# A Mamba-MLP block and a ternary FFN on one core: where the low bits of the FFN weights are summed, and how the last tile ends

## The reference

```python
def block(x):                       # first half
    xn = rmsnorm(x)
    z, xbc, dt_raw = split(xn @ w_in)            # 512, 768, 8 columns
    xc = silu(conv1d_4_taps(xbc) + conv_b)       # xh (512), B (128), C (128)
    dt = softplus(dt_raw + dt_bias)
    a = dt * -exp(a_log)
    # chunks: within a chunk masked exp(segsum(a)) * (C B^T) @ (dt*xh),
    # between chunks a state [heads, 64, 128] with decay
    y = y_diag + y_off + d_skip * xh
    g = rmsnorm(y * silu(z)) * norm_w
    h = x + g @ w_out
    return h + square(relu(rmsnorm(h) @ w_fc)) @ w_proj
def ffn(x):                         # ternary weights times scales per output row
    h = silu(w1(x)) * w2(x)         # 256 -> 1024
    h = gelu(h1(h)); h = gelu(h2(h))  # 1024 -> 1024, twice
    return w3(h)                    # 1024 -> 256
x = layernorm(x + block(x))
return layernorm(x + ffn(x))
```

## Time and profile before

| | |
|---|---|
| median of three timed executions | 1258.24 us (1256.99 to 1261.23) |
| the profiled execution, its own time | 1263.54 us |
| span in that profile | 1261.59 us |
| TensorE busy | 1209.6 us (96%) |
| VectorE busy | 797.7 us (63%) |
| ScalarE busy | 643.5 us (51%) |
| GpSimd busy | 249.8 us (20%) |
| mean granted clock of TensorE | 0.988 |

### The profile page before, as it was taken

The page is one execution under the profiler, slowest core; times in us unless marked ns, Lnnn a source line. Parts: engine busy times, 40 slices in busy tenths (PEclk is TensorE's granted clock), DMA queues, the critical chain, the costliest instruction groups (busy, mean ns, idle before and its releaser), DMA issues.

```text
span 1261.6 us, 19157 instructions
## 1 busy us (share of the span) xinstructions
PE 1209.6 (96%) x6452; PEld 1014.9 (80%) x6452; DVE 797.7 (63%) x1399; ACT 643.5 (51%) x1232; POOL 249.8 (20%) x215
## 2 busy tenths in 40 slices
PE   6779999999999999989999999999999999999996
PEld 4567887878787888878888888888888888888885
DVE  6898898988888898974624536336354263452633
ACT  5758787878787887756414214133241241422410
POOL 0445344342616253530000000000000000000000
PEclk9889999999999999999999999999999999999998
DMA  8111303131222220213800100101001010010000
GB/s 301 52 63 41 111 19 94 57 110 56 88 78 87 71 85 33 102 34 108 337 1 1 34 1 4 29 0 33 0 0 33 0 33 0 0 33 0 17 1 18
DMA packets 31112, 68.37 MB, mean 54 GB/s; under 512 B 3936, under 2 KB 22496, under 8 KB 29152
## 3 DMA queue, kind: packets, MB, share of 16 engines
q1 hardware_dynamic: 31072, 67.84, 15.7%
HBM read 59.43 MB, written 22.03 MB: 65 GB/s over the span
## 4 chain that ended last, share of the span: by engine, by line
issue 52%; POOL 0%; DVE 0%; POOLq 0%; DVEq 0%
POOL rsv_b L1771 0%; DVE o_sb L1842 0%; POOLq L1769 0%; DVEq L1623 0%; POOL rsv L234 0%; POOLq L434 0%
## 5 line engine op out<-in xcount | busy, mean ns | idle before, releaser
L1757 ACT ACTIVATE full<-bank,scale 128x512 f32<-128x512 f32 x128 | 88.3, 690 | 384.0 <-PE bank L1669 384.0
L1669 PE MATMUL bank<-hB_lo,h_sb 128*128 128x512 f32 x512 | 200.2, 391 | 0.0
L1669 PE MATMUL bank<-hB_hi,h_sb 128*128 128x512 f32 x512 | 199.7, 390 | 0.0
L1669 PE MATMUL bank<-hA_hi,h_sb 128*128 128x512 f32 x512 | 199.3, 389 | 0.0
L1669 PE MATMUL bank<-hA_lo,h_sb 128*128 128x512 f32 x512 | 199.3, 389 | 0.0
L1817 DVE CAST hA_hi<-full 128x512 fp32r<-128x512 f32 x64 | 27.3, 427 | 185.8 <-ACT full L1757 185.8
L1771 POOL TENSOR_TENSOR rsv_b<-mv_b,eps 128x4 f32<-128x4 f32 x8 | 10.7, 1339 | 624.9 <-DVE mv_b L186 624.9
L1669 PEld LDWEIGHTS bank<-hA_lo,h_sb 128*128 128x128 f32 x512 | 96.1, 188 | 20.1
L1669 PEld LDWEIGHTS bank<-hA_hi,h_sb 128*128 128x128 f32 x512 | 96.1, 188 | 20.1
L1669 PEld LDWEIGHTS bank<-hB_hi,h_sb 128*128 128x128 f32 x512 | 96.2, 188 | 19.2
L1669 PEld LDWEIGHTS bank<-hB_lo,h_sb 128*128 128x128 f32 x512 | 96.2, 188 | 19.1
(11 more groups left out here) (214 smaller groups left out, 3035.9 us busy)
## 6 DMA issues: line engine op xcount, KB each, us to landing
chk_xh<-w_ffn SPq DMA_DIRECT2D x16, 704.0 KB, 4.1
ffn_raw<-w_ffn SPq DMA_DIRECT2D x8, 1408.0 KB, 8.0
h_sb<-ffn_raw SPq DMA_DIRECT2D x2, 4096.0 KB, 19.5
xT<-x_t SPq DMA_DIRECT2D x8, 512.0 KB, 4.8
x_res<-x SPq DMA_DIRECT2D x8, 512.0 KB, 3.9
x_rows<-x SPq DMA_DIRECT2D x8, 512.0 KB, 3.4
x_in<-x_rows SPq DMA_DIRECT2D x8, 512.0 KB, 4.4
out<-o_sb SPq DMA_DIRECT2D x8, 512.0 KB, 3.2
```

The costliest lines, as they stand in the source:

```text
L1669: ins = pe.matmul(o, a_, b_, start=first and n == 0, stop=last and n == 1, skip_group_check=True)
L1757: nc.scalar.activation(full[:, n % FULL, :], b[:], ACT.Gelu, scale=scale[:, 1 + n // KH, n % KH:n % KH + 1]).then_inc(s_gd, 1)
```

## The change

VectorE's `low_bits` and its semaphore are gone. ScalarE's `low_sum` reads the low 16 bits of each word itself, as an unsigned 16-bit view with a stride of two over a whole half (128 x 1408), waits for the DMA of the half, and is called twice a pass: before yT(1), after the first projection of xbc, and before fc(7), after gate_rms(2). Each sum covers what four instructions (two masks, two sums) did. The sum now takes 16 low bits where 12 were masked before. `load_half` waits for one sum per half instead of two. lowsum has 16 columns instead of 32.

For the last tile of the FFN, TensorE issues the last two channels (j = 6, 7) of w3 first for chunks 0 and 1 and then for 2 and 3; `finish_last` of VectorE takes each accumulator as it is ready; and SyncE stores the last tile in two DMAs of two chunks each. `layer_norm_tail` is the old layer norm without its first part, split out so that `finish_last` can call it.

```diff
 def load_half(n, at):
-    ge(sp, s_sum, 2 * n)
+    ge(sp, s_sum, n)
     sp.dma_start(chk, w_ffn[:, bass.ds(at, PART)]).then_inc(s_chk, 16)
...
 def low_sum(i, n):
-    act.wait_ge(s_low, CHECKS * i + n + 1)
-    part = chk[:, n % HALVES * LOW:(n % HALVES + 1) * LOW]
-    nc.scalar.activation(part, part.bitcast(I32), ACT.Copy,
-                         accum_out=lowsum[:, bass.ds(CHECKS * i + n, 1)]).then_inc(s_sum, 1)
+    act.wait_ge(s_chk, 16 * HALVES * i + 16 * n + 16)
+    part = chk.bitcast(U16).rearrange("p (n b) -> p n b", b=2)[:, :, 0]
+    nc.scalar.activation(part, part, ACT.Copy,
+                         accum_out=lowsum[:, bass.ds(HALVES * i + n, 1)]).then_inc(s_sum, 1)
...
-def low_bits(i, n):
-    if n % HALVES == 0:
-        dve.wait_ge(s_chk, 32 * i + 16 * (n // HALVES) + 16)
-    part = chk[:, n % HALVES * LOW:(n % HALVES + 1) * LOW].bitcast(I32)
-    nc.vector.tensor_scalar(part, part, LOW_BITS, None,
-                            ALU.bitwise_and).then_inc(s_low, 1)
...
 store(TILES - 2, (TILES - 2) * TILE * D)
-store(TILES - 1, (TILES - 1) * TILE * D)
-sp.wait_ge(s_store, 16 * TILES + 1)
+i = TILES - 1
+for n in range(2):
+    r = slice(2 * n, 2 * n + 2)
+    sp.wait_ge(s_o, CH * i + 2 * n + 2)
+    sp.dma_start(rows(out, i * TILE * D)[:, r, :], o_sb[:, r, :]).then_inc(s_store, 16)
+sp.wait_ge(s_store, 16 * (TILES + 1) + 1)
...
-for j in range(KH - BEHIND, KH):
-    out_rows(j)
+if more:
+    for j in range(KH - BEHIND, KH):
+        out_rows(j)
+else:
+    for j in range(KH - BEHIND, KH - 2):
+        out_rows(j)
+    for half in (range(0, CH // 2), range(CH // 2, CH)):
+        for j in range(KH - 2, KH):
+            out_rows(j, half)
...
+def finish_last(i):
+    step = Steps(dve, s_bstep, B_STEPS * i)
+    dve.wait_ge(s_store, 16 * i + 1)
+    for n in range(2):
+        r = slice(2 * n, 2 * n + 2)
+        o = o_sb[:, r, :]
+        dve.wait_ge(s_acc, KH * i + KH + 2 * n)
+        nc.vector.tensor_tensor(o, acc[n][:].rearrange("p (c n) -> p c n", c=2),
+                                s3_b[:].unsqueeze(1).broadcast_to([P, 2, D]), ALU.mult).then_inc(s_accd, 1)
+        dve.wait_ge(s_accd, 2 * i + n + 2)
+        step.link(nc.vector.tensor_tensor(o, o, x1_res[:, r, :], ALU.add))
+        for c in range(2 * n, 2 * n + 2):
+            step.mark(nc.vector.bn_stats(bn_b[:, c, :], o_sb[:, c, :]))
+    step.wait(step.n)
+    layer_norm_tail(step, bn_b, mv_b, EPS_LN).then_inc(s_mvb, 1)
...
```

More of the change, by code:

```diff
@@ L22 @@
 BF16 = mybir.dt.bfloat16
+U16 = mybir.dt.uint16
 ALU = mybir.AluOpType
@@ L45 @@
 EPS_LN = 1e-05
-LOW_BITS = 0xFFF
 FAR = 1e30
@@ L99 @@
 FFN_WORDS = (2 * KD + 2 * KH) * HID + KH * D
-CHECKS = 4
 class Where:
@@ L140, in post_ln_block @@
     PART = PIECE // HALVES
-    LOW = PIECE // CHECKS
-    assert PIECE * TILES == FFN_WORDS and LOW * CHECKS == PIECE and CHECKS == 2 * HALVES
+    assert PIECE * TILES == FFN_WORDS and PART * HALVES == PIECE
     w_head, w_first = Where(HEAD, 0, ()), Where(FIRST, 0, (HEAD,))
@@ L178, in layer_norm_stats, with layer_norm_tail @@
             step.wait(step.n)
+            return layer_norm_tail(step, bn, mv, eps)
+        def layer_norm_tail(step, bn, mv, eps):
             tt, ts = nc.vector.tensor_tensor, nc.vector.tensor_scalar
@@ L259, in post_ln_block @@
         eps = sb("eps", [P, 4])
-        lowsum = sb("lowsum", [P, TILES * CHECKS])
+        lowsum = sb("lowsum", [P, TILES * HALVES])
         low_all = sb("low_all", [P, 1])
@@ L420, in post_ln_block @@
         s_raw = sem("ffn_piece_stored")
-        s_low = sem("low_bits_ready")
         s_sum = sem("low_bits_summed")
@@ L990, in iteration @@
                     yT(w, 0)
-                    low_sum(i, 0)
                     if more:
@@ L1004, in iteration @@
                         xbc(w, i + 1, 0)
-                    low_sum(i, 1)
+                    low_sum(i, 0)
                     yT(w, 1)
@@ L1017, in iteration @@
                         fc_square(w, i - 1, 6)
-                    low_sum(i, 2)
                     yT(w, 2)
                     gate_rms(step, w, i, 2)
-                    low_sum(i, 3)
+                    low_sum(i, 1)
                     if mlp:
@@ L1401, in iteration @@
                     mask_exponents(w, 0)
-                    if mlp:
-                        low_bits(i, 0)
                     mask_exponents(w, 1)
@@ L1408, in iteration @@
                         x_plus_h(i - 1, before)
-                        low_bits(i, 1)
                     y_diag(step, w, i, 0)
@@ L1417, in iteration @@
                     y_off(w, i, 1)
-                    if not mlp:
-                        low_bits(i, 0)
                     if more:
@@ L1449, in iteration @@
                         tap(step, w, i + 1, 4, 0)
-                    low_bits(i, 2)
                     if more:
                         tap(step, w, i + 1, 0, 0)
-                    low_bits(i, 3)
                     if more:
@@ L1568, in _ @@
                 iteration(w_last, TILES - 1, w_loop(TILES - 2), False, True)
-                dve.wait_ge(s_sum, CHECKS * TILES)
+                dve.wait_ge(s_sum, HALVES * TILES)
                 nc.vector.reduce_sum(low_all[:], lowsum[:], AX.X).then_inc(s_all, 1)
@@ L1689, in channel, with out_rows @@
                         last.then_inc(s_gi, 1)
-                    def out_rows(j):
+                    def out_rows(j, chunks=range(CH)):
                         pe.wait_ge(s_split, 3 * KH * i + 2 * KH + j + 1)
@@ L1694, in out_rows @@
                             pe.wait_ge(s_accd, 2 * i + 1)
-                        for c in range(CH):
+                        for c in chunks:
                             tok = slice(c * P, (c + 1) * P)
@@ L1821, in tile @@
                             turned_lo(dve, i + 1)
+                def finish_last(i):
[13 more added lines that the diff above has]
+                    layer_norm_tail(step, bn_b, mv_b, EPS_LN).then_inc(s_mvb, 1)
+                    dve.wait_ge(s_rsb, i + 1)
+                    for c in range(CH):
+                        nc.vector.tensor_scalar(o_sb[:, c, :], o_sb[:, c, :], mv_b[:, 0, c:c + 1], rsv_b[:, c:c + 1],
+                                                ALU.subtract, ALU.mult).then_inc(s_o, 1)
                 def finish(i, more):
@@ L1850, in _ @@
                 tile(TILES - 1, False, False)
-                finish(TILES - 1, False)
+                finish_last(TILES - 1)
 def kernel(**inputs):
```

## The result

The changed kernel takes 1253.83 us (median of 8, 1251.0 to 1255.67), the kernel before on the same chips 1259.01 (median of 8): ratio 0.9948, 95% interval 0.9934 to 0.9962, which is 6.5 us faster (4.8 to 8.3). Forecast were 4.75 us and 1253.5 us.

The account below looks back on a forecast made before the run. TensorE was taken to bound the steady passes, other engines mattering only where it waits. Terms 1.45 (steady passes) + 0.3 (diagonal products) + 0 (ScalarE) + 1.7 (pass 0) + 1.3 (end) = 4.75 us off 1258.24 give 1253.5; range 1250.1 to 1257.5.

Parts of the forecast that it names:

- the steady passes: Passes 2 to 6: without the mask, scores, loads and broadcast move 0.29 us earlier each, 1.45 us in all.
- the end: Last FFN tile: tail starts 0.65 us earlier and the store in two parts saves 0.65, together 1.3 us.
- pass 0: Without masks among the taps, yT_lo ends at 85.18 instead of 86.90; gain 1.7 us, ends 0.7 and 2.1.
- My upper end of 0.59: Steady passes: 0.59 us in each of five passes, 2.9 us in all, if GpSimd gives way.
- Pass 1 and y_diag: Pass 1 gains nothing; diagonal products' waits of up to 0.3 us are swallowed by line 612, except 0.3 in the last pass.
- 1408 take 1.37 us: ScalarE's new sum over 1408 half words takes 1.37 us, at 0.83 ns an element; covered, so it costs 0.
- the rival's threshold: ScalarE becomes late: above 2.1 us a sum, fc7's bank comes late and TensorE waits in seven passes; chance 0.05.
- The rival by which less waiting keeps the clock: Pass 0: with 3.5 us idle TensorE's clock may stay at 2.4 GHz, 1.2 us more, time 1252.3; chance 0.08.
- my lower end: Pass 0: gain only 0.7 us if GpSimd's long product gets in ahead of both taps.
- VectorE's wait for the broadcast: Sign in the changed profile: this wait grows from 2.4 to over 4 us.
- masks were covered: Steady passes give nothing and pass 0 gives 0.7; sum 2.3 us, time 1255.9; chance 0.27.
- only the end moves: Only the last tile's 1.3 us remain, every gain of a pass being lost again later; time 1256.9; chance 0.10.

Follow-up runs that it names:

- e4: Changed kernel with the two VectorE masks among the taps of pass 0 put back, in pass 0 alone; ratio 0.996 to the kernel before.
- e5: Changed kernel with the copy of the weight piece issued behind the load of the second half, not right behind the broadcast; 1248.78 us, ratio 0.9895.
- e9: Kernel before, with all masks, four sums a pass and old end, and only the weight-piece copy issued behind the second half's load; 1252.49 us, ratio 0.9936.
- e12: Changed kernel with the first sum on adjacent 16-bit numbers, the second on 32-bit words, and the flag set to zero; one execution, 1258.95 us, no ratio.
- e8: Changed kernel with ScalarE's second sum of each pass done twice; 1269.86 us, ratio 1.0071.
- e2: Kernel before with the new end alone, all masks and all four sums of a pass kept; ratio 0.9988.
- e3: Changed kernel with the first VectorE mask of a pass put back in passes 1 to 7, ahead of x_plus_h; ratio 0.9967.
- e1: Changed kernel with the old end of the last FFN tile (split order, finish_last and two stores taken back); 1255.96 us, ratio 0.9969.
- e10: Changed kernel with the late weight-piece copy and GpSimd's long product of pass 0 behind VectorE's last hT; 1247.85 us, ratio 0.9894.

## Why the prediction was right, and where not

The total came out (4.75 us forecast; 5.2 by the medians, 6.5 by the ratio). Its terms for the steady passes and the end are borne out by the traces. Its largest single term, pass 0, is not, so that the total fits so well is in part luck.

**The steady passes: right in mechanism and step, one link missing.** x_plus_h and the loads behind it moved by 0.28 us a pass (0.29 forecast), through GpSimd's turn, as said: the ud product fell from 1.33 to 1.04 us and the scores again started in as the second product ended (315.60 with 1.35 us, product to 315.87). My upper end of 0.59 could not have come whatever GpSimd did: y_off moved by 0.37 us only (from 7.11 to 6.74 us after the start of the pass), since it now waits 0.28 us for TensorE. That one side waits out the other's whole instruction is seen best in pass 0: in e4 the product ran to 81.36, and the tap behind it, 0.74 us alone, ended at 81.91. This fits the exclusive lock that the Trainium skill states (SBUF — State Buffer, section SBUF: two separate sides). The row of norms did land right behind xT (323.69 and 323.52). Of the 0.28 us some 0.2 arrive at the broadcast's issue.

What I missed is what comes after the issue. I took the broadcast's own 5.2 us as given. It is 3.1 to 3.8 us with nothing behind it (e5, e9) and 3.3 to 5.6 with the 1408 KB copy 0.4 to 0.6 us behind it, and this differs from pass to pass and from execution to execution of one kernel. In the profiled pair it was 0.88 us a pass shorter after than before, 5.3 us in six passes; that is most of what the spans differ by beyond the medians, and by the table above it does not belong to the change. Another 1.5 us is one pass of the kernel before, in which the granted clock was 0.5 from 404.3 to 407.7. That fall came right behind the pass's wait of 1.31 us on line 612, and no other trace shows one in passes 1 to 6; whether a shorter wait would have spared it is not shown. The sum was right because it was made from the 0.29 us and not from the whole wait of the earlier trace rows.

**Pass 1 and y_diag.** I gave pass 1 nothing, since VectorE "waits there for TensorE anyway". That holds: x_res is issued 10.03 us after the start of pass 1 in both profiles. That TensorE's wait there fell from 1.3 to 0.2 us goes with a landing of 3.5 us instead of 4.8. But I took the 0.3 us at y_diag for swallowed in steady passes. It is swallowed only where the broadcast is late; where it is quick, it is what the masks cost (e9: 2.2 us in seven waits). In passes 1 to 6 that is a gain of up to 1.7 us that the sum left out, and the ratio of 0.9948 (6.5 us, at least 4.8) leaves room for it.

**ScalarE: right result, wrong size.** "1408 take 1.37 us" was a term of the sum carried over from 32-bit rows. It took 1.80, as e12 shows for 16 bit with stride alone. The zero stands because the cover was 1.3 us, of which 1.0 were used up. I put the rival's threshold at 2.1 us a sum; e8 shows that the threshold is real and stands at 2.1 to 2.3 us.

**Pass 0: right step, a gain that is not shown.** yT_lo ended 1.76 us earlier in the pass (1.7 forecast), and the wait was 3.8 us (3.5 forecast). But the pass became only 0.9 us shorter. TensorE's granted clock was 0.5 for 6.8 us from 82.7, where it had been 0.5 for 3.4 us from 86.8. The rival by which less waiting keeps the clock went the other way round here. In e2, e4 and e9 the product was ahead of both taps, which was my lower end. Over all traces pass 0 is no shorter without the masks than with them (68.4 us in the mean, see e4), and e4's time (1.5 us) is not clear of nothing. So of the 1.7 us of this term anything from 0 to 1.7 is possible. The step that fails is "so it arrives": what yT_lo gains early in the pass does not show in the length of the pass. In the profiled pair the lower clock can account for a part of it; over all traces the cause is not shown.

**The end: right.** 1.17 us against 1.3. VectorE's part gave 0.49 (from the last matmul's end to the scaling, 5.97 us before and 5.48 after) where 0.65 was put: the second half's multiply at 1242.14 waits for the statistics of the first. The store by halves gave 0.67 (2.96 us from the last scaled element to landing before, 2.29 after) where 0.65 was put. By the fixed 2.0 us of the Trainium skill (DMA: Bandwidth & Descriptors, Anatomy of one DMA) it would have been 0.45. The skill gives that figure for transfers that GpSimd issues. These are issued by SyncE, and 2 KB landed in 1.4 us here, so the figure does not carry over.

**Of the signs named,** VectorE's wait for the broadcast did not grow but fell, from 14.5 us in six waits to 9.9. The fall is the shorter landing. With the copy late, where the landings are alike, the wait is 5.2 us in six passes with the masks (e9) and 5.6 without (e5). It did not grow because VectorE's new idle time lies earlier in the pass (0.28 us at line 1328 and 0.97 at line 1336), where it waits for TensorE. The rival "masks were covered" is not borne out, since the trace of e3 shows their cost at y_diag and at x_plus_h (its time alone does not prove it); "only the end moves" fell with e1.

**Open:** how the copy lengthens the landing of the broadcast, and why by so different an amount from pass to pass; the size of the gain in pass 0; and why the stretch from pass 7 to the FFN took 93.7 us in one trace of the changed kernel and 97.0 in the other.

## What to carry to other kernels

Where an engine waits for a transfer, look not only at what is queued ahead of it but at what is issued right behind it: a large copy that nobody waits for may move behind the next load for nothing, and here that gave at least as much as taking 32 masks off VectorE. A profile of one execution can be off from the median by luck of such landings; before a difference of two profiles is explained, compare the durations of what the edit did not touch. A gain inside a pass is a gain only once the length of the pass shows it, in more than one trace. And an engine that takes over work costs nothing only as long as its cover lasts, so measure the new form of the instruction before the next step.

## What the runs showed of the hardware

- A broadcast of a 2 KB row to 128 partitions (256 KB) lands in 3.1 to 3.8 us with nothing behind it (passes 1 to 6 of e5, e9 and e10) and in 3.3 to 5.6 with a copy of 1408 KB within DRAM issued 0.4 to 0.6 us behind it on the same queue. In pass 0, where no copy follows, it took 3.0 to 4.1 us over all traces. That the later transfer reaches into the earlier one fits the Trainium skill (DMA: Bandwidth & Descriptors, section Two DMAs through the same engine are not ordered), by which the descriptors of a queue start in order but are pipelined.
- ScalarE's accumulating copy of 1408 elements takes 1.37 us on int32, 1.38 on adjacent uint16 and 1.80 on uint16 four bytes apart.
- GpSimd's product of 128x2048 held up a VectorE tap, 0.74 us alone, to 4.8 us in e2, e4 and e9 and to 5.0 us in the kernel before; the product had started 0.25 to 0.34 us ahead of it. Which of the two came first differed between executions of the same lines.
